# Expert slots of a mixture-of-experts kernel: rows loaded as 32x32 blocks and transposed on VectorE

## What is computed

```python
x = x + tanh(g_xattn) * xattn(ctx, layernorm(x), mask, mask, ...)      # 32 x 128 x 128
xf = layernorm(x).reshape(-1, 128)                                     # 4096 rows
probs = softmax(xf @ router_w.T)                                       # 8 experts
topv, topi = top_k(probs, 2);  topv = topv / (topv.sum(-1) + 1e-9)
h = gelu(einsum('td,edh->teh', xf, w1))                                # 128 -> 512, per expert
y = einsum('teh,ehd->ted', h, w2)                                      # 512 -> 128
x = x + tanh(g_ffn) * (sum of topv * y over the two experts chosen)
```

## Time and profile before

| | |
|---|---|
| median of 3 runs | 340.66 us (340.45 to 340.80) |
| profiled execution, whole | 339.91 us |
| its span | 338.1 us |
| TensorE busy | 297.4 us, 88% |
| VectorE busy | 214.0 us, 63% |
| ScalarE busy | 192.4 us, 57% |
| GpSimd busy | 202.1 us, 60% |
| mean granted TensorE clock | 0.978 of the full 2.4 GHz |

### The profile page before, as it was taken

One profiled execution on the slowest core, in us unless ns is written; L12 is line 12 of the kernel. 1 busy time (PEld: TensorE's weight loads), 2 busy tenths in 40 slices (PEclk: granted clock), 3 DMA queues, 4 the chain that ended last, 5 costly groups with the idle time before them and its releaser, 6 DMA issues.

```text
span 338.1 us, 10971 instructions
## 1 busy us (share of the span) xinstructions
PE 297.4 (88%) x3633; PEld 266.6 (79%) x3633; DVE 214.0 (63%) x909; ACT 192.4 (57%) x472; POOL 202.1 (60%) x267
## 2 busy tenths in 40 slices
PE   1989999999999999997949997998999999999910
PEld 1777777787877878785738987998999999999910
DVE  2457577679888887889657796335843433335553
ACT  3166757868686886867685437546444444444300
POOL 3433233243586877857464788878878865655750
PEclk9999999999999999999998999999999999999985
DMA  7525521213042211751143222311452432248346
GB/s 226 154 85 168 162 92 33 80 37 95 25 116 69 61 54 49 225 162 31 49 109 94 65 69 83 81 47 55 105 120 87 132 102 72 64 137 286 98 127 187
DMA packets 41237, 34.61 MB, mean 102 GB/s; under 512 B 5044, under 2 KB 36950, under 8 KB 41184
## 3 DMA queue, kind: packets, MB, share of 16 engines
q1 hardware_dynamic: 33152, 23.62, 25.1%
q0 software_dynamic: 4320, 8.47, 7.0%
q10 hardware_dynamic: 3712, 1.84, 1.9%
HBM read 22.35 MB, written 12.01 MB: 102 GB/s over the span
## 4 chain that ended last, share of the span: by engine, by line
PE 72%; DVE 8%; issue 6%; ACT 5%; DMA 4%; POOL 3%; SPq 1%; POOLq 0%; ACTq 0%; DVEq 0%
PE ps_sc L1554 18%; PE ps_proj L1567 9%; PE ps_o L1567 8%; PE ps_o L1513 4%; PE ps_proj L1442 4%; PE ps_proj L1445 3%; PE ps_sc L1395 3%; PE ps_sc L1407 3%; PE ps_sc L1390 3%; PE ps_tail L1498 2%; PE ps_xT L1436 2%; ACT xr L772 2%; PE ps_tail L1489 2%; PE ps_proj L1459 2%; PE ps_o L1454 1%
## 5 line engine op out<-in xcount | busy, mean ns | idle before, releaser
L653 POOL DMA_INDIRECT picked<-yo,xg x71 | 72.2, 1016 | 16.5 <-issue 11.9
L1554 PE MATMUL ps_sc<-xt,w1c 128*128 128x128 f32 x568 | 76.3, 278 | 1.2 <-ACT xt L795 0.9
L635 POOL DMA_INDIRECT rows<-xr,posi x64 | 63.4, 990 | 18.0 <-issue 18.0
L1554 PEld LDWEIGHTS ps_sc<-xt,w1c 128*128 128x128 f32 x568 | 69.9, 194 | 2.2 <-ACT xt L795 1.3
L804 ACT ACTIVATE probT<-ps_sc 128x512 f32<-128x512 f32 x71 | 42.4, 597 | 43.8 <-PE ps_sc L1554 43.8
L1188 DVE TENSOR_REDUCE rowmax<-ps_sc 128x4 f32<-128x512 f32 x64 | 43.6, 690 | 24.8 <-PE ps_sc L1411 20.6
L698 ACT ACTIVATE probT<-ps_sc,pencol 128x512 f32<-128x512 f32 x64 | 43.6, 683 | 20.5 <-PE ps_sc L1411 18.3
L583 POOL TENSOR_TENSOR kblk<-kT,headcol 128x256 f32<-128x256 f32 x32 | 19.7, 614 | 54.3 <-ACT kT L730 54.1
L1567 PE MATMUL ps_proj<-w2s,probT 128*128 x288 | 38.5, 277 | 0.0
L1567 PE MATMUL ps_o<-w2s,probT 128*128 x280 | 37.0, 275 | 0.0
L1306 DVE COPY w1c<-w1s 128x512 f32 x71 | 31.4, 445 | 7.8 <-issue 2.8
(11 more groups left out here) (164 smaller groups left out, 587.2 us busy)
## 6 DMA issues: line engine op xcount, KB each, us to landing
xg<-rows SPq DMA_DIRECT2D x71, 65.0 KB, 1.8
ctxs<-ctxT SPq DMA_DIRECT2D x32, 128.0 KB, 2.1
xs<-x SPq DMA_DIRECT2D x8, 256.0 KB, 3.0
maskbc<-mask SPq DMA_DIRECT2D x8, 256.0 KB, 4.0
w1s<-w SPq DMA_DIRECT2D x4, 512.0 KB, 3.9
w2s<-w SPq DMA_DIRECT2D x8, 256.0 KB
maskbc<-picked SPq DMA_DIRECT2D x4, 512.0 KB, 6.6
out<-xs ACTq DMA_DIRECT2D x6, 256.0 KB, 2.3
```

What stands on the lines that cost most here:

```text
L635: nc.gpsimd.indirect_dma_start(out=rows, out_offset=bass.IndirectOffsetOnAxis(ap=posi[:, i, pick, b:b + 1], axis=0), in_=xr[:, i, pick, b, ...
L653: nc.gpsimd.indirect_dma_start(out=picked, out_offset=bass.IndirectOffsetOnAxis(ap=xg[:, r, D + 1:D + 2].bitcast(I32), axis=0), in_=yo[:, ...
L1554: last = nc.tensor.matmul(ps_score[j % DEEP][:, c * 128:(c + 1) * 128], w1c[:, j % DEEP, c * 128:(c + 1) * 128], xt[:, j % XRING, :], star ...
```

## The change

The load of a slot brings its rows to SBUF as 16 blocks of 32x32, in such an order that the transposes of the single blocks are the transpose of the whole. The four DMAs of a load each fill 32 partitions (a strip) with 32 columns of all 128 rows: 32 partitions x 4 blocks x 32 floats. A fifth brings the two last columns, weight and destination, to a new tile `xm`. DVE transposes the 16 blocks with one instruction from `xg` to `xt`, ahead of its copy of `w1c`, once all five have landed (LOADS). TensorE's transposes, their two PSUM buffers `ps_x` and ACT's copies are left out.

```diff
+LOADS = QUADS + 1
...
-        xg = sb("xg", [128, RING, ROW])
+        xg = sb("xg", [128, RING, D])
+        xm = sb("xm", [128, RING, 2])
...
-                sp.dma_start(xg[:, r, :], rows[bass.ds(at, 128), :]).then_inc(f_load[r], 16)
+                mine = rows[bass.ds(at, 128), :]
+                for strip in strips:
+                    sp.dma_start(xg[strip, r, :].rearrange("t (c d) -> t c d", c=QUADS),
+                                 mine[:, strip].rearrange("(c t) d -> t c d", c=QUADS)).then_inc(f_load[r], 16)
+                sp.dma_start(xm[:, r, :], mine[:, D:ROW]).then_inc(f_load[r], 16)
...
-                        ap=xg[:, r, D + 1:D + 2].bitcast(I32), axis=0),
+                        ap=xm[:, r, 1:2].bitcast(I32), axis=0),
...
-                j = slot_of(n, 0)
-                if j is not None:
-                    act.wait_ge(f_xT, j + 1)
-                    wait(act, f_up, j - XRING + 1)
-                    nc.scalar.activation(xt[:, j % XRING, :], ps_x[j % 2][:, 0:128],
-                                         ACT.Copy).then_inc(f_xt, 1)
...
+                    dve.wait_ge(f_load[j % RING], 16 * LOADS * (j // RING + 1))
+                    wait(dve, f_up, j - XRING + 1)
+                    nc.vector.transpose(xt[:, j % XRING, :], xg[:, j % RING, :]).then_inc(f_xt, 1)
...
-                    nc.vector.tensor_scalar(yo[:, r, :], ps_y[j % 2][:, 0:D], xg[:, r, D:D + 1], None,
+                    nc.vector.tensor_scalar(yo[:, r, :], ps_y[j % 2][:, 0:D], xm[:, r, 0:1], None,
...
-                j = slot_of(n, 0)
-                if j is not None:
-                    r = j % RING
-                    pe.wait_ge(f_load[r], 16 * (j // RING + 1))
-                    wait(pe, f_xt, j - 1)
-                    nc.tensor.transpose(ps_x[j % 2][:, 0:128], xg[:, r, 0:D], ident[:, :]).then_inc(f_xT, 1)
```

More of the change, by code:

```diff
@@ L319, in ps_turned @@
             return ps_xT if STEPS.index((G + LAG_OUT, 0)) < MIXED else ps_tail
-        ps_x = [ps_xT, ps_sc[:, 1024:1536]]
         s_ident = sem("s_ident")
@@ L395, in gated_cross_attention_moe @@
         f_load = [sem(f"f_load{i}") for i in range(RING)]
-        f_xT = sem("f_xT")
         f_xt = sem("f_xt")
```

## The result

The changed kernel takes 419.87 us (median of 4 runs, 418.95 to 420.46) against 340.73 us before (4 runs): the ratio is 1.234, 95% interval 1.228 to 1.239. The profiled execution took 419.74 us for a span of 417.9.

What follows compares the result with a forecast made beforehand. TensorE bounded the kernel (1.89 us a slot); SP's issuing, 0.82 + 4 x 0.57 = 3.10 us a slot, would take over, putting the last load at 393.7 and the span's end at 426.4: 427 us forecast, range 390 to 460.

Steps and rivals of the forecast that it cites:

- SP becomes the pace: Slot part, first load to last: SP's issuing takes 3.10 us a slot against the 1.89 us TensorE needs; chance 80%.
- The price of an added issue: SP's four added DMA issues per slot, 284 in all: 0.57 us each, with 0.40 to 0.68 kept as range.
- The stations: Times along SP's order: first pad 269.3, after pads 300.7, loads' end 393.7, first gather landed 398.2, last product 410.9, end 426.4.
- Ring and pad waits: SP's waits for ring places (35.0 us) and pad addresses (20.1 us) disappear; the last scatter wait should go too.
- DVE's transposes: 71 transposes on DVE at 0.3 us, 21 us in all, waiting about 1 us for the load in most slots.
- Rival 1: SP's added issues cost 0.27 us or less, TensorE keeps the pace and the change gains: 333 us; chance 4%.
- Rival 2: Slot loads: small packets at about 82 ns are the bound, 3.7 us a slot, 470 us; decides from 69 ns; chance 8%.
- Rival 3: TensorE, pausing in every slot, falls to its lower clock: 3.4 us a slot, up to 450 us; chance 8%.
- the stall of slot 66: DVE's first add waits for a gather issued only behind load 70: a stall of over 8 us.
- the tail: Behind the last load, 33 us to the end; a short low-clock spell after DVE's stall costs 1 to 2 us.
- The rule against cutting a transfer into partition parts: Slot loads: parts use the same 16 engines, so the cut was assumed to gain nothing in transfer.
- A cushion of 20 us ahead of need: SP's last load, issued at 293.3 and used at 315.1: 22 us of cushion, used up with 78 us more.

Runs made afterwards that it cites:

- the run with one load: Changed kernel with each slot's load as one DMA again, DVE's transpose kept, block arrangement left out: 335.18 us, ratio 0.988 against the kernel before.
- the small packets in one DMA: Changed kernel with its four strip DMAs replaced by one of 128 partitions x 4 pieces, xm's DMA kept, pieces from other columns: 337.18 us, ratio 0.993.
- the two-strips run: Changed kernel with only the first two of the four strip DMAs and xm, three DMAs a slot, half of the features left out: 356.20 us.

## Why the prediction was right, point by point

427 us was forecast, 419.87 measured, and the way there held step by step. That the two are so near is in part luck: one term was too long by 20 us, and what was left out made up for 12 of them. With the measured 0.50 for an added issue the same sum gives 408.

- *SP becomes the pace:* shown. Five issues on TensorE's path cost the same loss (420.2), one issue with everything else of the change costs none (335.2), and between them the time follows the count.
- *The price of an added issue* was the term that was mis-sized: 0.57 forecast, 0.50 measured. I had let a third dimension lengthen the DMA instruction, as in the load of xs in the earlier trace rows; the strips' instruction took 0.317. By 0.07 x 284 that is 20 us too much. What I had left out gave 12 of them back: a smooth slot is 2.82 us, but from load 41 (298.04) to the end of the last load (386.2) 30 slots take 2.94 each. Over all loads, 13 of the 355 DMA instructions took 0.5 to 1.7 us, 8 us too long together; nine pauses of SP of 0.34 us, one every 24 us or so, made some 2.6 more.
- *The stations:* first pad at 269.3 forecast, 266.3 measured; load 41 at 300.7, 298.0; end of loads 393.7, 386.2; first gather landed 398.2, DVE's add at 390.3, 4.1 behind the last issue where I had 4.5; last product 410.9, 402.7; end 426.4, 417.9. Behind the loads it took 31.7 us, where I had 32.7.
- *Ring and pad waits go:* shown by SP's waits. One of the three waits for scatters went too.
- *DVE's transposes*: 0.311 us, I had 0.3; at no cost of their own (the run with one load). Their waits I had at 1 us each and as the greatest of the trace; they are 2.1 us each, and ACT's wait for TensorE is greater. TensorE is busy for 75%, I had near 70.
- *Rival 1, hidden issues:* below 0.27 us an issue it would have been so; none here is that short from start to start (0.50 us), though the DMA instruction of a strip was shorter than any that I had rows of. Its 333 us is near what one issue gives, 335.2.
- *Rival 2, packets:* refuted by the small packets in one DMA; 22.5 ns a packet on SP's queue, far from the 69 from which it decides.
- *Rival 3, the clock:* it did fall, and cost nothing there. Windows of the changed kernel, a full one and a low one, and the one around the end of the stall:

```profile
303.10:340.50 37.40, 25.13 (x202) 23.19 (x201) 10.82 (x36) 7.16 (x12) 13.19 (x19) 1.00 0.24 45
340.60:343.90 3.30, 3.30 (x18) 3.30 (x18) 0.95 (x4) 0.60 (x1) 1.43 (x2) 0.50 0.29 62
381.60:395.10 13.50, 3.44 (x16) 3.47 (x17) 4.00 (x11) 0.60 (x1) 2.73 (x3) 0.50 0.60 182
```

Busy for two thirds, TensorE had the full clock of 2.4 GHz for 37 us, then the half for 3.3, in which it was busy all the time, and was up again; SP went on issuing in between and waited for nobody. In the stall of slot 66 the clock was low from 381.6 us on, and for 4.8 us behind it, to 395.1. TensorE behind the stall:

```profile
391.66 2.04 PE L1548 MATMUL ps_sc<-xt,w1c 128*128 128x128 f32 x8 [13.14 <-DVE xt L1304]
393.50 1.87 PE L1561 MATMUL ps_o<-w2s,probT 128*128 x8
395.20 1.06 PE L1548 MATMUL ps_sc<-xt,w1c 128*128 128x128 f32 x8
...
396.99 1.06 PE L1548 MATMUL ps_sc<-xt,w1c 128*128 128x128 f32 x8
```

Two products took 3.54 us there (391.66 to 395.20) and the next two 1.79 (to 396.99), so the low clock adds at most 1.8 us to the tail, where I had put 1 to 2.
- *The rule against cutting a transfer into partition parts* (the Trainium skill, DMA: Bandwidth & Descriptors, Rules for kernel authors) led the right way. The trace agrees: a strip landed 1.7 us after its issue, a whole load with four times the bytes 1.8, so the cut gains nothing in transfer. What it cost, though, was the issues, and not the shared engines that the Trainium skill gives as the reason.

Left open: what makes a DMA instruction now and then up to five times as long, and why one of 64 partitions takes longer than one of 32 or of 128. Spreading the issues over ACT's queue was not tried; three left on SP would, by the two-strips run, still lose 16 us.

## What to carry to other kernels

Before a transfer is cut into more DMAs, multiply the time from one issue to the next on the issuing sequencer, register work included, by the number of DMAs in a period, and set it against the period of the engine that is the bound; the page shows no busy time for that sequencer, only its timeline and the chain do. A cushion of 20 us ahead of need says nothing about a pace: at the new pace it never formed here, and DVE's transposes waited for their loads from the first slots on. And look in the issuer's order for what stands behind the delayed transfers, since it is delayed with them.

## What was not expected of the hardware

The time that a DMA instruction holds SP differed with its partitions, and not in order: 32 partitions 0.317 us (with 128-byte pieces) and 0.316 (512-byte rows), 64 partitions 0.61 and 0.48, 128 partitions 0.38 and 0.33 (520-byte rows). And packets of 128 bytes were cheap: with 512 of them in one DMA a slot the kernel took 337.18 us, and DVE's transposes waited 5.7 us in all for their loads; the mean packet of SP's queue fell from 41 to 22.5 ns.
